# Masked copies of two experts in one VectorE instruction, in the first mixture of a two-layer kernel

## The chip, the cores and the metric

The kernel runs on one core of a Trainium2 chip. Its time is the device time of one execution in microseconds (us). Five engines work beside one another and meet through semaphores: TensorE (PE; PEld is its weight load), VectorE (DVE), ScalarE (ACT), GpSimd (POOL) and SyncE (SP), which here issues DMAs.

## What is computed

Two layers on 16 sequences of 512 tokens of 128 features. Each layer adds a gated sequence block and then a gated mixture of experts to its input, each behind a layer norm with shift and scale. The change lies in the mixture of the first layer: eight experts, one for each token.

```python
h = _layernorm(x) * (1 + cb) + sb
logits = h @ gate_w + gate_b
sel = argmax(softmax(logits))                 # one of 8 experts for each token
onehot = one_hot(sel, 8)
y_all = einsum('td,edh->eth', h, expert_w) + expert_b[:, None, :]
x = x + gb * einsum('te,eth->th', onehot, y_all)
```

## The kernel before

The kernel runs in stages with a barrier of all engines between them. The stage of the first mixture works on 16 tiles w (`B` = 16), each of 512 tokens (`C` = 4 chunks of `P` = 128 tokens). It has no loop for them: for every engine the order of its steps is written out, as `mask(0, 0); mask(0, 1); ...`, and each step waits on semaphores for what it needs. An engine does its steps strictly in that order.

For a tile the steps are these. VectorE (`statistics`, `gamma`, `joined`) and ScalarE and GpSimd (`norm_y`, `beta`, `means`, `scales`) finish the block before it and the norm; TensorE transposes the normed tokens (`turn`), ScalarE adds shift and scale and leaves the features in `f_t` (`feat`, 128 features x 512 tokens, fp32). TensorE makes the eight logits (`logits`), VectorE finds the largest and writes one-hot rows `hot` (`best`), TensorE transposes them (`turn_hot`), ScalarE writes them as `hot_b`, and SyncE sends them to DRAM and back, spread over all 128 partitions, as `wide` (128 x 8 experts x 512 tokens, bf16: one or zero for each expert and token).

Then come the masked copies and their products. `mask(w, e)` on VectorE multiplies `f_t` of the tile by the row of expert e in `wide` and writes `masked`, 128x512 fp32: the tokens of other experts are zero. `product(w, e)` on TensorE multiplies it by the weights of expert e and adds up all eight in one bank of PSUM, behind `bias(w)`. A product of fp32 is two passes, so 128 products are 256 matmul records. ScalarE scales the sum (`scaled`, into `moe_t`), TensorE transposes it back (`turn_back`), and VectorE adds it to `x_tok` (`added`).

`masked` is a ring of four buffers of one expert. `mask(w, e)` waits by `expert(dve, "product", w, e - 4)` until the product that read the same buffer last is done, and `product(w, e)` waits until the count of `masked` has passed w * 8 + e. `feat` and `spread` also wait for the last masked copy of the tile four before, as `f_t` and `wide` have four buffers.

The order of TensorE puts transposes, logits and the bias between the products, for instance `product(12, 5); product(12, 6); turn_hot(14); turn(15); product(12, 7); bias(13); logits(15); product(13, 0)`, and `turn_hot(w)` waits for `best(w)`.

Of the kernel before, what the change touches and what calls it, by code (L numbers as in the profile page):

```python
# [18 lines left out]
C = 4  # L19
# [18 lines left out]
def build(nc, a, out):  # L38
# [8 lines left out]
    with ctx:  # L47
        def sb(name, shape, dt=F32, scope=ctx):
            names_used.append(name)
            return scope.enter_context(nc.sbuf_tensor(f"{name}_{len(names_used)}", shape, dt))  # L50
# [662 lines left out]
        with ExitStack() as sc:  # L713
# [18 lines left out]
            hot_b = [sb(f"hot_b{w}", [K3, C * P], BF16, scope=sc) for w in range(W)]  # L732
            wide = [sb(f"wide{w}", [P, E, C * P], BF16, scope=sc) for w in range(W)]
            moe_t = [sb(f"moe_t{w}", [P, C * P], scope=sc) for w in range(2)]
            masked = [sb(f"masked{m}", [P, C * P], scope=sc) for m in range(4)]
            logit = sb("logit", [P, C, E], scope=sc)
            top = sb("top", [P, C, 8], scope=sc)
            idx = sb("idx", [P, C, 8], U32, scope=sc)
# [40 lines left out]
            def expert(eng, name, w, e):  # L779
                w, e = w + e // E, e % E  # L780
                if exists(w):
                    eng.wait_ge(s[name], w * E + e + 1)

            with nc.Block() as block:
# [201 lines left out]
                def _(dve):  # L986
                    def statistics(w):
                        done(dve, "y_sq", w - 1)
                        for c in range(C):
                            last = nc.vector.bn_stats(halves[:, c, :], features_of(w * C + c))  # L990
                        last.then_inc(s["y_sum"], 1)
                        done(dve, "y_sum", w)
                        for c in range(C):
                            last = nc.vector.bn_aggr(moments[:, w * C + c, :], halves[:, c, :])
                        last.then_inc(s["y_sq"], 1)

                    def stats_x(w):
                        done(dve, "joined", w)
                        done(dve, "stats_x", w - 1)
                        for c in range(C):  # L1000
                            last = nc.vector.bn_stats(halves_x[:, c, :], x_tok[:, w * C + c, :])
                        last.then_inc(s["sum_x"], 1)
                        done(dve, "sum_x", w)
                        for c in range(C):
                            last = nc.vector.bn_aggr(moments_x[:, w * C + c, :], halves_x[:, c, :])
                        last.then_inc(s["stats_x"], 1)
# [5 lines left out]
                    def gamma(w):  # L1012
                        if w < HEAD:
                            done(dve, "y_sq", w)
                            landed(dve, s_rows, w)
                            for c in range(C):
                                t = w * C + c
                                last = nc.vector.scalar_tensor_tensor(yn[w % 2][:, c, :], features_of(t), moments[:, t, 0:1], rows[w % W][:, 0, :], ALU.subtract, ALU.mult)
                            last.then_inc(s["gamma"], 1)
                        elif exists(w):  # L1020
                            done(dve, "y_normed", w)
                            landed(dve, s_rows, w)
                            nc.vector.tensor_tensor(yn[w % 2][:, :, :], yn[w % 2][:, :, :], rows[w % W][:, 0:1, :].to_broadcast([P, C, D]), ALU.mult).then_inc(s["gamma"], 1)

                    def joined(w):
                        if exists(w):
                            done(dve, "gamma", w)
                            done(dve, "beta", w)
                            if w < HEAD:
                                done(dve, "root_y", w)  # L1030
                                for c in range(C):
                                    t = w * C + c
                                    last = nc.vector.scalar_tensor_tensor(x_tok[:, t, :], yn[w % 2][:, c, :], rs_y[:, t:t + 1], x_tok[:, t, :], ALU.mult, ALU.add)
                            else:
                                for c in range(C):
                                    t = w * C + c
                                    last = nc.vector.scalar_tensor_tensor(x_tok[:, t, :], x_tok[:, t, :], 1.0, yn[w % 2][:, c, :], ALU.mult, ALU.add,
                                                                          accum_out=sum_x[:, t:t + 1])
                            last.then_inc(s["joined"], 1)
# [29 lines left out]
                    def mask(w, e):  # L1069
                        if e == 0:  # L1070
                            landed(dve, s_wide, w)
                            done(dve, "feat", w)
                        expert(dve, "product", w, e - 4)
                        nc.vector.tensor_tensor(masked[e % 4][:, :], f_t[w % W][:, :], wide[w % W][:, e, :], ALU.mult).then_inc(s["masked"], 1)  # L1074

                    dve.wait_ge(s["down"], 1)
                    statistics(0); statistics(1); gamma(0); joined(0); stats_x(0); gamma(1); shift_x_head(0); joined(1); stats_x(1)
                    statistics(2); shift_x_head(1); gamma(2); joined(2); best(0); stats_x(2); statistics(3); shift_x_head(2); best(1)
                    gamma(3); joined(3); stats_x(3); statistics(4); shift_x_head(3); mask(0, 0); mask(0, 1); mask(0, 2); mask(0, 3)
                    mask(0, 4); mask(0, 5); mask(0, 6); best(2); mask(0, 7); mask(1, 0); mask(1, 1); mask(1, 2); mask(1, 3); gamma(4)  # L1080
                    mask(1, 4); mask(1, 5); added(0); joined(4); mask(1, 6); mask(1, 7); statistics(5); statistics(6); statistics(7)
                    best(3); mask(2, 0); mask(2, 1); mask(2, 2); mask(2, 3); mask(2, 4); added(1); gamma(5); mask(2, 5); joined(5)
                    mask(2, 6); mask(2, 7); gamma(6); best(4); mask(3, 0); mask(3, 1); mask(3, 2); joined(6); mask(3, 3); mask(3, 4)
                    mask(3, 5); mask(3, 6); mask(3, 7); gamma(7); added(2); joined(7); statistics(8); best(5); mask(4, 0); mask(4, 1)
                    mask(4, 2); mask(4, 3); mask(4, 4); mask(4, 5); added(3); mask(4, 6); best(6); mask(4, 7); gamma(8); joined(8)
                    statistics(9); mask(5, 0); mask(5, 1); best(7); mask(5, 2); mask(5, 3); mask(5, 4); added(4); mask(5, 5); mask(5, 6)
                    mask(5, 7); mask(6, 0); mask(6, 1); gamma(9); mask(6, 2); joined(9); mask(6, 3); best(8); mask(6, 4); added(5)
                    mask(6, 5); statistics(10); mask(6, 6); mask(6, 7); mask(7, 0); mask(7, 1); statistics(11); mask(7, 2); best(9)
                    gamma(10); joined(10); mask(7, 3); mask(7, 4); added(6); mask(7, 5); mask(7, 6); mask(7, 7); mask(8, 0); mask(8, 1)
                    mask(8, 2); gamma(11); joined(11); mask(8, 3); mask(8, 4); mask(8, 5); added(7); statistics(12); mask(8, 6); best(10)  # L1090
                    mask(8, 7); mask(9, 0); mask(9, 1); mask(9, 2); statistics(13); gamma(12); joined(12); best(11); mask(9, 3); mask(9, 4)
                    added(8); mask(9, 5); mask(9, 6); mask(9, 7); mask(10, 0); mask(10, 1); mask(10, 2); gamma(13); joined(13); mask(10, 3)
                    mask(10, 4); mask(10, 5); best(12); added(9); statistics(14); mask(10, 6); mask(10, 7); mask(11, 0); mask(11, 1)
                    mask(11, 2); mask(11, 3); statistics(15); best(13); gamma(14); joined(14); mask(11, 4); added(10); mask(11, 5)
                    mask(11, 6); mask(11, 7); mask(12, 0); mask(12, 1); mask(12, 2); gamma(15); joined(15); mask(12, 3); mask(12, 4)
                    added(11); mask(12, 5); mask(12, 6); mask(12, 7); mask(13, 0); best(14); mask(13, 1); mask(13, 2); mask(13, 3); best(15)
                    mask(13, 4); mask(13, 5); added(12); mask(13, 6); mask(13, 7); mask(14, 0); mask(14, 1); mask(14, 2); mask(14, 3)
                    mask(14, 4); mask(14, 5); added(13); mask(14, 6); mask(14, 7); mask(15, 0); mask(15, 1); mask(15, 2); mask(15, 3)
                    mask(15, 4); mask(15, 5); added(14); mask(15, 6); mask(15, 7); added(15)

                @block.tensor
                def _(pe):
# [38 lines left out]

                    def product(w, e):
                        expert(pe, "masked", w, e)
                        nc.tensor.matmul(ps[:, w % 2, :], ew0[:, e, :], masked[e % 4][:, :], start=False, stop=(e == E - 1)).then_inc(  # L1144
                            s["product"], 1)

                    pe.wait_ge(s["weights"], 6 * 16)
# [1580 lines left out]
```

## Time and profile before

| | |
|---|---|
| three runs, us | 952.89, 949.35, 950.57 (median 950.57) |
| the profiled execution, us | 948.88 |
| its span, first to last instruction, us | 947.1 |
| mean granted TensorE clock | 0.937 of full speed |
| busy share: TensorE, VectorE, ScalarE, GpSimd | 88%, 82%, 66%, 60% |
| masked copies (line 1074), VectorE | 128, from 175.2 us to 332.4 us |
| products (line 1144), TensorE | 256 passes, 122.8 us busy |

The profile is of one execution. Times are us from its first instruction, unless marked ns. Busy time is the time in which an engine had an instruction under way. A timeline row merges like instructions: its start, the time from the first's start to the last's end, the engine, line, operation, tiles written and read, how many there are, and in brackets how long the engine stood idle before it and who released it. Successive instructions of VectorE are drawn as overlapping a little, and those of TensorE by more.

### The profile page before, as it was taken

The numbers are of one execution on the slowest core, as the hardware profiler recorded it, in microseconds if no ns is written. First come the engines' busy times: TensorE is split into PE (matmuls) and PEld (weight loads), VectorE is DVE, ScalarE is ACT, GpSimd is POOL, SyncE is SP. The second block draws the span as 40 slices with busy tenths as digits, with TensorE's granted clock in tenths as the row PEclk, the third lists the DMA queues.
The fourth block names the chain that finished last, engine by engine and source line by source line (L and its number), as shares of the span: only waits on it lengthen the run. The fifth ranks groups of instructions, "written<-read, shape, count | busy, mean of one in ns | idle before, by whom it ended". The sixth has DMA issues, their size and how long they took to land.

```text
span 947.1 us, 23545 instructions
## 1 busy us (share of the span) xinstructions
PE 833.6 (88%) x7422; PEld 645.5 (68%) x7422; DVE 775.4 (82%) x2369; ACT 629.4 (66%) x1620; POOL 570.3 (60%) x551
## 2 busy tenths in 40 slices
PE   6878892898999948999999999999729999999990
PEld 6855571444454427888888888888517888888880
DVE  3988778999999747678999999999886866666996
ACT  3567123488788365567777777766566888888880
POOL 1211004297776325343788888888777777777773
PEclk9999796799999978999999999999858999999996
DMA  5330362232322202000011111111117666756987
GB/s 155 94 95 1 90 181 63 101 145 102 146 96 90 90 25 68 2 1 10 30 36 44 39 35 37 38 36 45 44 55 219 204 208 181 223 182 195 348 250 252
DMA packets 83462, 100.79 MB, mean 106 GB/s; under 512 B 15326, under 2 KB 65305, under 8 KB 81164
## 3 DMA queue, kind: packets, MB, share of 16 engines
q1 hardware_dynamic: 71388, 79.61, 27.3%
q0 software_dynamic: 8640, 17.97, 5.3%
q10 hardware_dynamic: 3312, 1.70, 0.6%
q8 instruction: 62, 1.02, 0.5%
q14 instruction: 60, 0.49, 0.2%
HBM read 75.71 MB, written 23.54 MB: 105 GB/s over the span
## 4 chain that ended last, share of the span: by engine, by line
PE 55%; DVE 4%; DMA 1%; issue 1%; SPq 1%; ACT 1%; POOL 0%; ACTq 0%; DVEq 0%
PE ps L2636 13%; PE ps L2393 12%; PE ps L2659 7%; PE ps L2409 4%; PE ps L2471 2%; PE ps L2384 2%; PE ps L2619 2%; PE ps L2404 2%; PE ps L2530 2%; PE ps L2510 2%; PE ps L2355 1%; PE ps L2370 1%; PE ps L2458 1%; PE ps L2654 1%; PE ps L2483 1%
## 5 line engine op out<-in xcount | busy, mean ns | idle before, releaser
L1579 POOL TENSOR_TENSOR kvb<-qk,v 128x1024 f32<-128x1024 f32 x64 | 126.2, 1976 | 74.9 <-DVE qk L1950 50.3
L1588 POOL DMA_INDIRECT rows_of<-payb,posu x128 | 145.5, 1137 | 40.3 <-issue 27.8
L2393 PE MATMUL ps<-con,kvb 128*128 128x128 f32 x1024 | 126.0, 276 | 0.0
L1144 PE MATMUL ps<-masked,ew 128*128 128x512 f32 x256 | 122.8, 609 | 2.0 <-DVE masked L1074 1.9
L2393 PEld LDWEIGHTS ps<-con,kvb 128*128 128x128 f32 x1024 | 119.4, 192 | 1.0 <-issue 1.0
L2315 DVE TENSOR_SCALAR qk<-ps,b 128x256 f32<-128x256 f32 x142 | 62.0, 478 | 49.3 <-PE ps L2636 44.4
L1612 POOL DMA_INDIRECT parts<-h,dest x72 | 81.0, 1125 | 22.0 <-issue 21.0
L1926 DVE TENSOR_TENSOR qc<-ps,qk 128x1024 f32<-128x1024 f32 x64 | 78.1, 1220 | 18.4 <-PE ps L2393 17.7
L1612 POOL DMA_INDIRECT parts<-gx,dest x70 | 79.3, 1133 | 21.3 <-issue 20.7
L1074 DVE TENSOR_TENSOR masked<-f_t,wide 128x512 f32<-128x512 f32 x128 | 87.2, 725 | 5.9 <-PE ps L1144 5.7
L1144 PEld LDWEIGHTS ps<-masked,ew 128*128 128x128 f32 x256 | 44.9, 192 | 44.3 <-issue 30.4
L2659 PE MATMUL ps<-w,f_t 128*128 x568 | 75.0, 275 | 0.0
L2659 PEld LDWEIGHTS ps<-w,f_t 128*128 128x128 f32 x568 | 69.0, 192 | 8.2
L1836 ACT ACTIVATE qk<-ps,b 128x256 f32<-128x256 f32 x142 | 59.6, 471 | 18.7 <-PE ps L2636 18.3
L2636 PE MATMUL ps<-qd,ex 128*128 128x256 f32 x288 | 70.4, 388 | 0.0
L2636 PE MATMUL ps<-qd,lg 128*128 128x256 f32 x280 | 66.2, 379 | 0.0
L2636 PEld LDWEIGHTS ps<-qd,ex 128*128 128x128 f32 x288 | 53.5, 196 | 6.1
L1841 ACT ACTIVATE nrm<-qk,limit 128x512 f32<-128x512 f32 x71 | 51.3, 722 | 6.8
L2204 DVE SCALAR_TENSOR_TENSOR f_t<-qk,nrm 128x512 f32<-128x512 f32 x71 | 49.2, 693 | 6.6 <-DVE qk L2315 0.4
L2636 PEld LDWEIGHTS ps<-qd,lg 128*128 128x128 f32 x280 | 50.5, 190 | 5.4
L908 ACT ACTIVATE junk<-x_tok,stat 128x128 f32<-128x128 f32 x112 | 43.3, 389 | 12.8 <-DVE x_tok L1065 11.0
L236 POOL TENSOR_SCALAR rstd<-mv 128x16 f32<-128x16 f32 x4 | 1.1, 276 | 58.8 <-DVE mv L256 58.8
(374 smaller groups left out, 2131.1 us busy)
## 6 DMA issues: line engine op xcount, KB each, us to landing
wide<-hot_dram SPq DMA_DIRECT2D x16, 1024.0 KB, 4.5
kvb<-rows_of SPq DMA_DIRECT2D x71, 132.0 KB, 3.4
ex<-in_w_dram SPq DMA_DIRECT2D x36, 256.0 KB
lg<-in_w_dram SPq DMA_DIRECT2D x35, 256.0 KB
toep<-taps_dram SPq DMA_DIRECT2D x16, 512.0 KB, 5.0
xg<-parts SPq DMA_DIRECT2D x16, 512.0 KB, 5.9
x_tok<-in_x_dram SPq DMA_DIRECT2D x16, 256.0 KB, 3.0
rows<-rows_dram SPq DMA_DIRECT2D x16, 192.0 KB, 3.1
```

The costliest lines, as they stand in the source:

```text
L1074: nc.vector.tensor_tensor(masked[e % 4][:, :], f_t[w % W][:, :], wide[w % W][:, e, :], ALU.mult).then_inc(s["masked"], 1)
L1144: nc.tensor.matmul(ps[:, w % 2, :], ew0[:, e, :], masked[e % 4][:, :], start=False, stop=(e == E - 1)).then_inc(s["product"], 1)
L1579: nc.gpsimd.tensor_tensor(kv[g % KB][:, :, :].rearrange("p e (h d) -> p e h d", h=H), k_in, v_in, ALU.mult).then_inc(s["kv"], 1)
L1588: nc.gpsimd.indirect_dma_start(rows_of, bass.IndirectOffsetOnAxis(ap=posu[w % PR][:, slot, t:t + 1], axis=0), pay[w % PB][:, t, :], None). ...
L1612: nc.gpsimd.indirect_dma_start(parts, bass.IndirectOffsetOnAxis(ap=dest[:, at, c:c + 1], axis=0), yw[u][:, c, :], None).then_inc(s_out[u], 16)
L1836: last = nc.scalar.activation(glu[v % 2][:, f, :], ps[:, bank, f * SP:(f + 1) * SP], ACT.Relu, bias=b1[:, bass.ds(e * NF + f, 1)], scale=-1.0)
L1841: nc.scalar.activation(gs[v % 2][:, :, :], glu[v % 2][:, :, :], ACT.Gelu_apprx_sigmoid, bias=limit[:, :], scale=-1.0).then_inc(m["gs"], 1)
L1926: nc.vector.tensor_tensor(qc[g % 2][:, :, :], cum(g), q_in, ALU.mult).then_inc(s["qc"], 1)
L2315: last = nc.vector.tensor_scalar(lin[v % 2][:, f, :], ps[:, bank + 1, f * SP:(f + 1) * SP], b1[:, bass.ds(e * NF + 2 + f, 1)], 8.0, ALU.ad ...
L2393: last = nc.tensor.matmul(cum(g)[:, e, :], kv[g % KB][:, e, :], k("upto"), start=True, stop=True)
L2636: last = nc.tensor.matmul(ps[:, bank + f // 2, (f % 2) * SP:(f % 2 + 1) * SP], w1c[v % WC][:, f * P:(f + 1) * P], x_t[v % 2][:, :], start= ...
L2659: last = nc.tensor.matmul(to, act_t[v % 2][:, j, c * P:(c + 1) * P], w2[:, bass.ds(e * (2 * D) + j * D, D)], start=False, stop=(c == S - 1 ...
```

## The change

`masked` becomes two buffers of two experts (the same memory), VectorE makes the copies of experts e and e + 1 with one instruction of 2 x 512 columns, where `f_t` is repeated by a broadcast and `wide` is read over both experts. It waits for the product of expert e - 3, the second reader of its pair buffer, and counts `masked` up by 2. `product(w, e)` reads half e % 2 of pair buffer e // 2 % 2; its wait is as it was. In VectorE's written order `mask(w, e)` with odd e is gone, and stands where its even neighbour stands; all other steps keep their order. TensorE's order is as it was.

```diff
-            masked = [sb(f"masked{m}", [P, C * P], scope=sc) for m in range(4)]
+            masked = [sb(f"masked{m}", [P, 2, C * P], scope=sc) for m in range(2)]
...
                         if e == 0:
                             landed(dve, s_wide, w)
                             done(dve, "feat", w)
-                        expert(dve, "product", w, e - 4)
-                        nc.vector.tensor_tensor(masked[e % 4][:, :], f_t[w % W][:, :], wide[w % W][:, e, :], ALU.mult).then_inc(s["masked"], 1)
+                        expert(dve, "product", w, e - 3)
+                        nc.vector.tensor_tensor(masked[e // 2 % 2][:, :, :], f_t[w % W][:, :].unsqueeze(1).to_broadcast([P, 2, C * P]),
+                                                wide[w % W][:, e:e + 2, :], ALU.mult).then_inc(s["masked"], 2)
...
-                    gamma(3); joined(3); stats_x(3); statistics(4); shift_x_head(3); mask(0, 0); mask(0, 1); mask(0, 2); mask(0, 3)
-                    mask(0, 4); mask(0, 5); mask(0, 6); best(2); mask(0, 7); mask(1, 0); mask(1, 1); mask(1, 2); mask(1, 3); gamma(4)
-                    mask(1, 4); mask(1, 5); added(0); joined(4); mask(1, 6); mask(1, 7); statistics(5); statistics(6); statistics(7)
-                    best(3); mask(2, 0); mask(2, 1); mask(2, 2); mask(2, 3); mask(2, 4); added(1); gamma(5); mask(2, 5); joined(5)
...
+                    gamma(3); joined(3); stats_x(3); statistics(4); shift_x_head(3); mask(0, 0); mask(0, 2)
+                    mask(0, 4); mask(0, 6); best(2); mask(1, 0); mask(1, 2); gamma(4)
+                    mask(1, 4); added(0); joined(4); mask(1, 6); statistics(5); statistics(6); statistics(7)
+                    best(3); mask(2, 0); mask(2, 2); mask(2, 4); added(1); gamma(5); joined(5)
+                    mask(2, 6); gamma(6); best(4); mask(3, 0); mask(3, 2); joined(6); mask(3, 4)
...
+                    mask(10, 4); best(12); added(9); statistics(14); mask(10, 6); mask(11, 0)
+                    mask(11, 2); statistics(15); best(13); gamma(14); joined(14); mask(11, 4); added(10)
+                    mask(11, 6); mask(12, 0); mask(12, 2); gamma(15); joined(15); mask(12, 4)
+                    added(11); mask(12, 6); mask(13, 0); best(14); mask(13, 2); best(15)
...
-                        nc.tensor.matmul(ps[:, w % 2, :], ew0[:, e, :], masked[e % 4][:, :], start=False, stop=(e == E - 1)).then_inc(
+                        nc.tensor.matmul(ps[:, w % 2, :], ew0[:, e, :], masked[e // 2 % 2][:, e % 2, :], start=False, stop=(e == E - 1)).then_inc(
                             s["product"], 1)
```

## Rows read from the trace of the kernel before

**Rows 1.** Busy time by stretch, all engines, with granted clock and DMA
```profile
core 0: us, PE busy (x) PEld busy (x) DVE busy (x) ACT busy (x) POOL busy (x), PEclk, DMA share, GB/s
...
182.00:229.00 47.00, 42.45 (x163) 21.63 (x161) 46.04 (x175) 35.96 (x113) 33.32 (x53) 1.00 0.28 104
229.00:298.00 69.00, 67.42 (x253) 33.48 (x252) 67.42 (x258) 55.25 (x172) 50.19 (x83) 1.00 0.30 115
298.00:310.00 12.00, 11.64 (x45) 6.00 (x44) 10.53 (x35) 10.90 (x40) 8.66 (x14) 1.00 0.22 88
310.00:335.00 25.00, 25.00 (x76) 11.48 (x75) 17.91 (x51) 7.73 (x29) 8.01 (x12) 1.00 0.23 85
```

**Rows 2.** Groups: busy us, mean ns, then idle before them and its releaser
```profile
L1144 PE MATMUL ps<-masked,ew 128*128 128x512 f32 x256 | 122.8, 609 | 2.0 <-DVE masked L1074 1.9
L1074 DVE TENSOR_TENSOR masked<-f_t,wide 128x512 f32<-128x512 f32 x128 | 87.2, 725 | 5.9 <-PE ps L1144 5.7
```

**Rows 3.** Waits, 170 to 340 us: us in total, times, longest
```profile
PEld ps L1144 <- DVE masked L1074: 13.5, 36, 1.5
...
DVE masked L1074 <- PE ps L1144: 5.7, 15, 1.5
```

**Rows 4.** Timeline, start of the masked copies
```profile
175.18 2.48 DVE L1074 TENSOR_TENSOR masked<-f_t,wide 128x512 f32<-128x512 f32 x4
...
175.91 10.30 PE L1144 MATMUL ps<-masked,ew 128*128 128x512 f32 x20 [1.41 <-DVE masked L1074]
...
182.14 3.09 DVE L1074 TENSOR_TENSOR masked<-f_t,wide 128x512 f32<-128x512 f32 x5
```

**Rows 5.** Timeline, end of the stage
```profile
310.21 0.69 DVE L1074 TENSOR_TENSOR masked<-f_t,wide 128x512 f32<-128x512 f32 x1 [1.47 <-PE ps L1144]
...
311.34 1.96 PE L1144 MATMUL ps<-masked,ew 128*128 128x512 f32 x4
...
329.34 0.60 PE L1132 MATMUL ps<-con,moe_t 128*128 128x128 f32 x4
...
329.78 5.32 PE L1144 MATMUL ps<-masked,ew 128*128 128x512 f32 x12
...
330.98 1.41 DVE L1074 TENSOR_TENSOR masked<-f_t,wide 128x512 f32<-128x512 f32 x2
```

**Rows 6.** Timeline, TensorE's bias and logits ahead of the product at 311.34 us
```profile
310.11 0.39 PE L1140 MATMUL ps<-hot_b,ebx 24*128 24x512 bf16 x1
310.42 1.06 PE L1116 MATMUL ps<-gw,f_t 128*128 128x8 f32 x8
```

**Rows 7.** Timeline, VectorE, first copies of tiles 5 and 12
```profile
229.00 1.26 DVE L1074 TENSOR_TENSOR masked<-f_t,wide 128x512 f32<-128x512 f32 x2
...
298.33 1.89 DVE L1074 TENSOR_TENSOR masked<-f_t,wide 128x512 f32<-128x512 f32 x3
```

**Rows 8.** Timeline, a run of copies that meets an idle TensorE
```profile
195.99 3.09 DVE L1074 TENSOR_TENSOR masked<-f_t,wide 128x512 f32<-128x512 f32 x5
...
196.73 2.84 PE L1144 MATMUL ps<-masked,ew 128*128 128x512 f32 x6
...
199.00 0.28 DVE L1065 SCALAR_TENSOR_TENSOR x_tok<-x_tok,ps 128x128 f32<-128x128 f32 x1
```

**Rows 9.** Groups of VectorE by form, whole kernel
```profile
L1950 DVE TENSOR_TENSOR qk<-qk,lg 128x1024 f32<-128x1024 f32 x16 | 19.6, 1225 | 0.5
...
L1023 DVE TENSOR_TENSOR yn<-yn,rows 128x512 f32<-128x512 f32 x12 | 8.4, 697 | 0.0
```

**Rows 10.** Timeline, a 1024-column product of VectorE and the instruction behind it
```profile
502.58 1.23 DVE L1926 TENSOR_TENSOR qc<-ps,qk 128x1024 f32<-128x1024 f32 x1
503.72 0.94 DVE L1932 RECIPROCAL rden<-ps 96x128 f32<-96x128 f32 x1
```

**Rows 11.** Timeline, copies beside an addition of GpSimd
```profile
207.65 5.24 DVE L1074 TENSOR_TENSOR masked<-f_t,wide 128x512 f32<-128x512 f32 x5
...
208.34 1.72 POOL L867 TENSOR_TENSOR x_tok<-x_tok,rows 128x512 f32<-128x512 f32 x1
```

More of the change, by code:

```diff
@@ L1082, in _ @@
-                    best(3); mask(2, 0); mask(2, 1); mask(2, 2); mask(2, 3); mask(2, 4); added(1); gamma(5); mask(2, 5); joined(5)
-                    mask(2, 6); mask(2, 7); gamma(6); best(4); mask(3, 0); mask(3, 1); mask(3, 2); joined(6); mask(3, 3); mask(3, 4)
-                    mask(3, 5); mask(3, 6); mask(3, 7); gamma(7); added(2); joined(7); statistics(8); best(5); mask(4, 0); mask(4, 1)
-                    mask(4, 2); mask(4, 3); mask(4, 4); mask(4, 5); added(3); mask(4, 6); best(6); mask(4, 7); gamma(8); joined(8)
@@ L1086, in _ @@
[L1086 to L1097, printed above, removed]
@@ L1098, in _ @@
-                    mask(14, 4); mask(14, 5); added(13); mask(14, 6); mask(14, 7); mask(15, 0); mask(15, 1); mask(15, 2); mask(15, 3)
-                    mask(15, 4); mask(15, 5); added(14); mask(15, 6); mask(15, 7); added(15)
+                    gamma(3); joined(3); stats_x(3); statistics(4); shift_x_head(3); mask(0, 0); mask(0, 2)
+                    mask(0, 4); mask(0, 6); best(2); mask(1, 0); mask(1, 2); gamma(4)
+                    mask(1, 4); added(0); joined(4); mask(1, 6); statistics(5); statistics(6); statistics(7)
@@ new lines, in _ @@
+                    best(3); mask(2, 0); mask(2, 2); mask(2, 4); added(1); gamma(5); joined(5)
+                    mask(2, 6); gamma(6); best(4); mask(3, 0); mask(3, 2); joined(6); mask(3, 4)
+                    mask(3, 6); gamma(7); added(2); joined(7); statistics(8); best(5); mask(4, 0)
+                    mask(4, 2); mask(4, 4); added(3); mask(4, 6); best(6); gamma(8); joined(8)
+                    statistics(9); mask(5, 0); best(7); mask(5, 2); mask(5, 4); added(4); mask(5, 6)
+                    mask(6, 0); gamma(9); mask(6, 2); joined(9); best(8); mask(6, 4); added(5)
@@ new lines, in _ @@
+                    statistics(10); mask(6, 6); mask(7, 0); statistics(11); mask(7, 2); best(9)
+                    gamma(10); joined(10); mask(7, 4); added(6); mask(7, 6); mask(8, 0)
+                    mask(8, 2); gamma(11); joined(11); mask(8, 4); added(7); statistics(12); mask(8, 6); best(10)
+                    mask(9, 0); mask(9, 2); statistics(13); gamma(12); joined(12); best(11); mask(9, 4)
+                    added(8); mask(9, 6); mask(10, 0); mask(10, 2); gamma(13); joined(13)
+                    mask(10, 4); best(12); added(9); statistics(14); mask(10, 6); mask(11, 0)
@@ new lines, in _ @@
+                    mask(11, 2); statistics(15); best(13); gamma(14); joined(14); mask(11, 4); added(10)
+                    mask(11, 6); mask(12, 0); mask(12, 2); gamma(15); joined(15); mask(12, 4)
+                    added(11); mask(12, 6); mask(13, 0); best(14); mask(13, 2); best(15)
+                    mask(13, 4); added(12); mask(13, 6); mask(14, 0); mask(14, 2)
+                    mask(14, 4); added(13); mask(14, 6); mask(15, 0); mask(15, 2)
+                    mask(15, 4); added(14); mask(15, 6); added(15)
```

## The prediction

> **What bounds the kernel now.** I read the busy time by stretch first [rows 1]. The change touches one stage, the first mixture of experts, whose masked copies run from 175.2 to 332.3 us. From 182 to 298 us VectorE is busy 46.04 of 47 us and then 67.42 of 69 us, while TensorE is busy 42.45 of 47 and 67.42 of 69. From 310 us on TensorE is busy all of the 25 us and VectorE only 17.91. So VectorE carries the stage up to about 308 us, TensorE is close behind, and the end is TensorE's: it runs without a gap up to the last product.
>
> The second view is the two groups that the change touches [rows 2]: 128 masked copies by VectorE, and the 256 TensorE passes (two for each product of an expert) that read them. The third is the waits [rows 3]: VectorE's copies waited for a product for only 5.7 us in all, 15 times. The timeline places these: all lie ahead of the copies that start at 182.14 us [rows 4] or from 308.7 us on, as the one of 1.47 us that ends at 310.21 [rows 5]. Between them VectorE never waited. TensorE's weight loads waited 13.5 us for masked copies, in 36 short pieces: there VectorE is the one that is late.
>
> TensorE's own floor is near. A product of one expert is 0.86 us (twelve passes from 329.78 us hold the engine for some 5.15 us, 0.43 each), a group of four transposes 0.43 (329.34 to 329.78) [rows 5], the bias 0.31 and the logits 0.92 [rows 6]. A tile of 512 tokens needs 8 x 0.86 + 3 x 0.43 + 0.31 + 0.92 = 9.4 us. VectorE gives it one each 9.9 us: the seven tiles from 229.0 to 298.3 us [rows 7].
>
> **What the change saves.** 128 copies of 512 columns become 64 of 1024. The five copies in a row from 195.99 us have the next instruction start at 199.00, so one costs 3.01 / 5 = 0.60 us [rows 8], though each is drawn 0.68 long: successive instructions overlap by 0.08. A product of 1024 fp32 columns, both inputs in SBUF, is drawn 1225 ns [rows 9]; the nearest case of what starts behind such a one is 502.58 to 503.72 us, 1.14 [rows 10]. So a pair costs 1.14 against 1.20, and saves 0.06 us. That one input is repeated by a broadcast costs nothing extra in the nearest row: the 512-column product with broadcast rows is drawn 697 ns, beside 725 for the copies [rows 2, 9]. By drawn durations alone the saving would be 2 x 0.68 - 1.225 = 0.14; I take 0.06, since the starts are what the engine's queue pays. Over the some 50 pairs ahead of 308 us: 50 x 0.06 = 3 us. Those behind it lie beside TensorE's work and save nothing.
>
> The Trainium skill ("VectorE: DVE Perf Modes", section on the TRN2 errata) says that an SBUF-source instruction pays a fixed cost each time, and gives an fp32 tensor_tensor as N + 151 cycles. This case's drawn durations agree (0.68 and 1.225 us), its start distances don't. By that rule a pair would save 151 cycles, 0.157 us, and the 50 pairs 7.9 us.
>
> **What the change adds: waits.** The four buffers of one expert become two of two. Three things change. (1) A product of an even expert now needs the whole pair: after an idle TensorE it starts 1.22 + 0.06 us behind the pair's start, where it started 0.68 + 0.06 behind the copy's (195.99 to 196.73) [rows 8]. (2) A pair needs both products of the pair two before; a copy needed the product four before. (3) Behind a product's end the copy starts 0.20 us later (product ends at 329.78 + 1.72 = 331.50; the second copy of the row at 330.98 starts at 331.70) [rows 5].
>
> Take a run of copies that meets an idle TensorE. Before: copy k could start at 0.60 k; the fifth, at 2.41, needs the product that ends at 0.74 + 0.86 + 0.20 = 1.80, and even the seventh, at 3.61, needs one at 3.52. Seven go through without a wait. After: the third pair could start at 2.28, and needs both first products: 1.28 + 1.72 + 0.20 = 3.20. It waits 0.92 us. The order written out for VectorE has such runs of three pairs or more in nearly all tiles, across the tile's edge too (copies 6, 7 of one tile and 0 to 3 of the next). Behind the waiting pair stand the normalisation, routing and residual work of later tiles, in VectorE's queue, and behind those ScalarE, GpSimd and TensorE's transposes. As VectorE is the bound, a wait there is paid in full.
>
> I walked the two queues of the new order by hand, with these prices, the other VectorE work between pairs taken as the distance of the rows of before, and the port collisions below kept as they are. The start: the first pair is done at 176.4, the first product starts 0.55 us later (it was at 175.91), and the pairs (0, 4) and (0, 6) wait for products until 179.7 and 181.4. Before, seven copies and the routing were done by 182.14 [rows 4], the copy (1, 0) started at 182.74, and now starts at about 183.9: 1.2 us late. Then the lateness of the first copy of each tile is 1.2 at tile 2, 1.9 at tile 3 (the run at 195.99: 0.9 wait), 1.6 at 4, 2.3 at 5 and at 6, 2.7 at 7, 2.5 at 8, 3.0 at 9, 4.1 at 10, 4.5 at 11, 5.2 at 12, and 6.9 at 13, where the pair waits for product (12, 5). That last wait holds back the routing of tile 14, for which TensorE's turn of the one-hot rows stands in line: some 2 us idle. TensorE starts product (13, 0) at about 318.0, before at 311.34 [rows 5]: 6.7 us late. In sum: 1.2 us at the start, some 9 us of waits of 0.3 to 1.2 us, less 3 saved.
>
> From there TensorE has no gap, and keeps none. With product (w, 0) at time 0 pair (w, 4) may start at 1.92 and is needed at 3.9, pair (w, 6) at 4.1 and needed at 5.6. The end of the stage is therefore 6.7 us late, and nothing behind its barrier is changed.
>
> **The forecast.** The profiled execution took 948.88 us, 947.1 of them its span; 948.9 + 6.7 = 955.6. The median of the three runs is 950.57, 1.7 above the profiled one; with that offset kept, and the walk's last tenths not to be trusted, I say 957.0.
>
> **Rivals.** *Waits half absorbed.* The walk takes each wait at full price; some fall where VectorE would wait for TensorE anyway, or the collisions fall on fewer instructions. Of 9 us of waits half is left: 1.2 + 4.5 - 3 = 2.7, 953.3 us. For it speaks that TensorE has only 0.5 us of slack in a tile, against it that VectorE never waited between 182 and 308 us.
>
> *VectorE alone decides: faster.* If TensorE always kept two pairs ahead, no pair would wait, and the start's 1.2 us less the 3 saved gives -1.8: 948.8. It decides where TensorE works off each pair before VectorE has made two more; the 3.20 against 2.28 us above speaks against it. For it speaks that three copies that stood behind other work (routing, statistics) now are made with their even neighbour, 2 to 4 us sooner.
>
> *The fixed cost is the drawn one: clearly faster.* With 0.14 instead of 0.06 a pair and no waits, 50 x 0.14 - 1.2 = 5.8 off: 944.8. TensorE's idle time in 182 to 310 us, 6.5 us by its busy time [rows 1], would just allow it. The rule of the page above would make it 7.9 - 1.2 = 6.7 off, 943.9.
>
> *The port: slower still.* The five copies from 207.65 took 5.24 us instead of 3.09: GpSimd's add of 1.72 us at 208.34 and a second one each held a copy back by 1.07 [rows 11]. I keep these holds. But GpSimd's small steps, which feed the norms and so TensorE's turns, also wait for the copy under way, and would now wait up to 1.14 instead of 0.60. Some three such steps on the way to a late turn are 1.6 us, at two or three tiles: 3 to 4 us more, 960.5. The Trainium skill ("SBUF — State Buffer", section "Who interferes with whom") has VectorE with two SBUF inputs and a reading GpSimd exclude each other for a whole instruction; the collision agrees. It speaks against this change.
>
> **Chances.** Forecast (954.5 to 959.5) 0.50; half absorbed (951 to 954.5) 0.22; VectorE alone 0.11; drawn fixed cost 0.05; port 0.12. The likeliest's own range is 954.5 to 959.5. For 8 in 10 I leave out the fast end and what lies above 962: 949.5 to 962. A measurement of this kernel tells some 0.5% from no change, 4.75 us: below 945.8 faster, above 955.3 slower. Faster 0.05; same 0.22 + 0.11 and the low end of the forecast, 0.08, together 0.41; slower 0.54.
>
> **What would show it.** In the new profile: 64 copies of 1024 columns drawn near 1.23 us; VectorE's waits for products at some 15 to 18 us instead of 5.7, and many of them between 190 and 308 us, right before third pairs; VectorE no longer at 98% there; TensorE's busy share between 182 and 298 lower, its last product near 341.7 us instead of 335; 25 dense us at the end as before. The prediction is wrong if pairs start closer than 1.1 us behind one another, if VectorE's waits stay under 8 us, or if TensorE's end moves without them, which would point to GpSimd.

## The result and the profile after

The changed kernel takes 965.64 us (median of four runs, 964.22 to 966.65) against 950.56 for the kernel before: ratio 1.0148, 95% interval 1.0126 to 1.017. It is slower by 15.1 us. The sign was as forecast and the forecast waits are there; the size was not: 957.0 was said, with 954.5 to 959.5 as its own range and 962 as the top of the wide one.

The profiled execution took 964.88 us, 963.1 of them its span. In it all lines behind the changed instruction are one higher (1145 for the products). Busy time by stretch of the kernel after, to be read beside [rows 1]:

```profile
core 0: us, PE busy (x) PEld busy (x) DVE busy (x) ACT busy (x) POOL busy (x), PEclk, DMA share, GB/s
...
175.00:182.00 7.00, 5.03 (x7) 2.27 (x8) 4.16 (x10) 3.74 (x8) 4.48 (x5) 0.50 0.42 151
182.00:229.00 47.00, 41.95 (x152) 20.71 (x150) 40.42 (x142) 31.21 (x96) 32.72 (x47) 0.99 0.28 93
229.00:298.00 69.00, 60.01 (x221) 30.76 (x220) 57.93 (x201) 49.57 (x158) 50.92 (x73) 0.98 0.29 106
...
310.00:335.00 25.00, 22.86 (x83) 11.28 (x82) 18.32 (x56) 16.18 (x57) 13.19 (x19) 1.00 0.29 105
335.00:355.00 20.00, 16.96 (x48) 7.20 (x46) 11.55 (x32) 6.54 (x26) 7.00 (x11) 1.00 0.07 29
```

No engine carries the stage any more. From 229 to 298 us VectorE is busy 57.93 us instead of 67.42 and TensorE 60.01 instead of 67.42; each waits for another. GpSimd did less of its work in that time and was as busy, 50.92 us after 50.19. The groups and the busy line of the whole kernel, and the waits from 170 to 355 us, of the kernel after [rows 2, 3]:

```profile
PE 835.6 (87%) x7422; PEld 645.5 (67%) x7422; DVE 769.3 (80%) x2305; ACT 629.5 (65%) x1620; POOL 583.6 (61%) x551
...
L1145 PE MATMUL ps<-masked,ew 128*128 128x512 f32 x256 | 124.7, 618 | 3.1 <-DVE masked L1074 2.8
...
L1074 DVE TENSOR_TENSOR masked<-f_t,wide 128x1024 f32<-128x1024 f32 x64 | 79.6, 1254 | 24.8 <-PE ps L1145 24.4
```

```profile
DVE masked L1074 <- PE ps L1145: 24.4, 31, 2.8
ACT yn L932 <- POOL stat L850: 16.9, 10, 4.5
...
PE ps L1125 <- DVE hot L1056: 7.5, 7, 1.9
...
PE ps L1109 <- ACT xn L942: 7.4, 6, 4.2
```

VectorE's masked copies now wait 24.4 us for products, 5.7 before. TensorE waits 7.4 us for normed tokens to transpose (2.9 before) and 7.5 for one-hot rows (2.9 before). ScalarE waits 16.9 us for GpSimd's statistics, 8.5 before.

The timeline of the kernel after has the forecast wait at the forecast place, the run of copies at the start of tile 2 [rows 8]. VectorE:

```profile
199.75 2.36 DVE L1074 TENSOR_TENSOR masked<-f_t,wide 128x1024 f32<-128x1024 f32 x2
203.12 1.23 DVE L1074 TENSOR_TENSOR masked<-f_t,wide 128x1024 f32<-128x1024 f32 x1 [1.01 <-PE ps L1145]
204.26 0.28 DVE L1065 SCALAR_TENSOR_TENSOR x_tok<-x_tok,ps 128x128 f32<-128x128 f32 x1
```

TensorE in the same stretch: the first product 1.28 us behind the pair's start.

```profile
201.03 2.84 PE L1145 MATMUL ps<-masked,ew 128*128 128x512 f32 x6 [0.45 <-DVE masked L1074]
```

A pair costs 204.26 - 203.12 = 1.14 us, as taken, and the third of a run waits 1.01 us, where 0.92 was worked out. Two other places cost more than the walk had. The first is the start, TensorE and VectorE [rows 4]:

```profile
177.18 10.01 PE L1145 MATMUL ps<-masked,ew 128*128 128x512 f32 x16 [1.98 <-DVE masked L1074]
```

```profile
175.91 2.35 DVE L1074 TENSOR_TENSOR masked<-f_t,wide 128x1024 f32<-128x1024 f32 x2
181.06 1.23 DVE L1074 TENSOR_TENSOR masked<-f_t,wide 128x1024 f32<-128x1024 f32 x1 [2.81 <-PE ps L1145]
183.87 1.23 DVE L1074 TENSOR_TENSOR masked<-f_t,wide 128x1024 f32<-128x1024 f32 x1 [1.58 <-PE ps L1145]
```

The second is a hole in TensorE at 267 to 271.7 us, which the kernel before did not have, and behind it a stretch at the lower clock:

```profile
265.52 1.98 PE L1145 MATMUL ps<-masked,ew 128*128 128x512 f32 x4
271.66 1.01 PE L1109 MATMUL ps<-con,xn 128*128 128x128 f32 x4 [4.16 <-ACT xn L942]
```

The granted clock in both, of the kernel after (the column behind the busy times; 0.50 is 1.2 GHz, 1.00 is 2.4 GHz):

```profile
179.00:183.00 4.00, 4.00 (x6) 1.66 (x5) 1.23 (x1) 2.09 (x4) 0.65 (x2) 0.50 0.01 2
183.00:186.00 3.00, 3.00 (x8) 1.31 (x7) 2.00 (x6) 0.00 (x0) 0.00 (x0) 1.00 0.00 0
267.00:271.00 4.00, 0.50 (x2) 0.00 (x0) 2.74 (x11) 3.11 (x14) 3.15 (x5) 1.00 0.71 250
271.00:275.00 4.00, 3.34 (x10) 2.36 (x11) 1.45 (x11) 3.79 (x15) 1.79 (x5) 0.59 0.13 47
```

### The profile page after: what moved, and what is told of

Read it like the earlier page. It is cut to its first block, busy times and chain, and to the rows that moved or that the text cites. A ratio compares the mean times of both kernels' runs of the same rounds, so it can differ in the third digit from the quotient of the medians.

```text
span 963.1 us, 23543 instructions
## 1 busy us (share of the span) xinstructions
PE 835.6 (87%) x7422; PEld 645.5 (67%) x7422; DVE 769.3 (80%) x2305; ACT 629.5 (65%) x1620; POOL 583.6 (61%) x551
## 3 DMA queue, kind: packets, MB, share of 16 engines
q8 instruction: 62, 1.02, 0.4%
## 4 chain that ended last, share of the span: by engine, by line
PE 54%; DVE 3%; DMA 2%; SPq 1%; issue 1%; ACT 1%; POOL 0%; ACTq 0%; DVEq 0%; POOLq 0%
PE ps L2637 13%; PE ps L2394 12%; PE ps L2660 7%; PE ps L2410 3%; PE ps L2472 2%; PE ps L2385 2%; PE ps L2620 2%; PE ps L2405 2%; PE ps L2531 2%; PE ps L2511 2%; PE ps L2371 1%; PE ps L2356 1%; PE ps L2459 1%; DMA parts<-gx,dest 1%; PE ps L2484 1%
## 5 line engine op out<-in xcount | busy, mean ns | idle before, releaser
L1074 DVE TENSOR_TENSOR masked<-f_t,wide 128x1024 f32<-128x1024 f32 x64 | 79.6, 1254 | 24.8 <-PE ps L1145 24.4
L1613 POOL DMA_INDIRECT parts<-gx,dest x70 | 79.8, 1140 | 21.3 <-issue 20.7
L908 ACT ACTIVATE junk<-x_tok,stat 128x128 f32<-128x128 f32 x112 | 43.3, 388 | 18.0 <-DVE x_tok L1065 12.7
```

Of the source, the lines that this page charges most:

```text
L1074: nc.vector.tensor_tensor(masked[e // 2 % 2][:, :, :], f_t[w % W][:, :].unsqueeze(1).to_broadcast([P, 2, C * P]), wide[w % W][:, e:e + 2, ...
L1613: nc.gpsimd.indirect_dma_start(parts, bass.IndirectOffsetOnAxis(ap=dest[:, at, c:c + 1], axis=0), yw[u][:, c, :], None).then_inc(s_out[u], 16)
```

## The experiments

The theories. (1) The ring: with two pair buffers VectorE waits for products, and pays. (2) The long instruction: 1024 columns hold GpSimd's steps back, and the norms they feed. (3) The start: a later first product and a later clock. (4) The order: odd copies made ahead of routing and statistics delay those. The measured times are medians; each ratio is against the kernel before, measured beside it (950.57, 950.58 or 951.33 us).

**e1: four pair buffers.**

```diff
-            masked = [sb(f"masked{m}", [P, 2, C * P], scope=sc) for m in range(2)]
+            masked = [sb(f"masked{m}", [P, 2, C * P], scope=sc) for m in range(4)]
...
-                        expert(dve, "product", w, e - 3)
+                        expert(dve, "product", w, e - 7)
...
```

The copy and the product index the buffer by `(w * E + e) // 2 % 4` with it.

> The changed kernel with four pair buffers instead of two (eight experts deep), so that a pair waits for the product seven before it and no longer for the pair two before; instructions of 1024 columns and the written order stay. If the waits on the ring of buffers are the cause (theory 1), VectorE's waits for products fall from 24.4 us to under 5 and the time is 947 to 952 us, the level of before. If the 1024-column instructions holding GpSimd back are it (theory 2), GpSimd's busy time stays some 13 us above before and the time stays above 957. If the late first product and the late TensorE clock are it (theory 3), some 3 us of the 15 remain: about 954.

Measured: 960.83 us, ratio 1.0103 (1.0073 to 1.0132). The waits of e1 from 170 to 360 us and its busy line:

```profile
ACT yn L932 <- POOL stat L850: 20.1, 10, 4.5
DVE x_tok L1065 <- PE ps L1133: 15.8, 8, 4.6
...
DVE logit L1044 <- PE ps L1117: 9.1, 7, 2.3
...
PE ps L1109 <- ACT xn L942: 8.4, 5, 3.6
...
DVE masked L1074 <- PE ps L1145: 0.5, 1, 0.5
```

```profile
PE 834.3 (87%) x7407; PEld 647.3 (67%) x7422; DVE 772.3 (80%) x2305; ACT 628.7 (66%) x1620; POOL 587.5 (61%) x551
```

The ring waits are gone, 24.4 to 0.5 us, and only 4.8 of the 15 us with them. Much of that waiting came back at other steps of VectorE: it now stands 15.8 us before `added` for transposes back (7.4 in the changed kernel) and 9.1 us before `best` for logits (0.4). What is left of the loss has theory 2's mark: ScalarE waits 20.1 us for GpSimd, and GpSimd is busy 587.5 us, 17 more than before.

**e2: the pair's instruction split in two again, all its waits kept.**

```diff
-                        nc.vector.tensor_tensor(masked[e // 2 % 2][:, :, :], f_t[w % W][:, :].unsqueeze(1).to_broadcast([P, 2, C * P]),
-                                                wide[w % W][:, e:e + 2, :], ALU.mult).then_inc(s["masked"], 2)
+                        nc.vector.tensor_tensor(masked[e // 2 % 2][:, 0, :], f_t[w % W][:, :], wide[w % W][:, e, :], ALU.mult)
+                        nc.vector.tensor_tensor(masked[e // 2 % 2][:, 1, :], f_t[w % W][:, :], wide[w % W][:, e + 1, :], ALU.mult).then_inc(s["masked"], 2)
```

> The changed kernel with each 1024-column instruction split again into two of 512, and everything else as changed: the waits of a pair, its two buffers, one count of 2 behind the second, the order. Theory 1 (ring waits): nothing is won, 965 to 968 us, as the 3 us of saved fixed cost are lost too. Theory 2 (long instructions hold GpSimd): GpSimd's busy time falls back by some 13 us, TensorE's wait of 4.2 us at 267 us goes, and the time is 957 to 960.

Measured: 964.09 us, ratio 1.0143 (1.0111 to 1.0176). Its busy line:

```profile
PE 835.9 (87%) x7407; PEld 645.9 (67%) x7422; DVE 774.8 (81%) x2369; ACT 630.2 (66%) x1620; POOL 569.8 (59%) x551
```

Theory 2's signs came: GpSimd is back at 569.8 us (570.3 before), and TensorE waits 1.05 us for the norm of tile 10 (at 268.74 us) where the changed kernel has 4.16. Its gain did not come: 1.5 us by the medians, with overlapping intervals. So the hole can go and the time stay: with two pair buffers the ring (and the order) are enough for nearly the whole loss.

**e3: one expert at a time with the waits of before, in the changed order.**

```diff
-                        expert(dve, "product", w, e - 3)
...
+                        for f in (e, e + 1):
+                            expert(dve, "product", w, f - 4)
+                            nc.vector.tensor_tensor(masked[f // 2 % 2][:, f % 2, :], f_t[w % W][:, :], wide[w % W][:, f, :], ALU.mult).then_inc(s["masked"], 1)
```

> One expert at a time again, with the waits and counts of before (product four before, one count each) in four single places, but in the changed order: the copy of the odd expert right behind its even neighbour. If the order is innocent (theories 1 and 2) the time is that of before, 948 to 953 us. If pulling the odd copies ahead of routing, statistics and residual steps delays those (theory 4), it is 955 or more.

Measured: 954.22 us over ten runs, ratio 1.0028 (1.0007 to 1.0049). It is between the two expectations: the order alone costs some 2.7 us by the ratio, 0.7 to 4.7 by its interval. VectorE waits 11.1 us for products in it, 5.7 in the kernel before.

**e4: tile 0 one by one, the rest as changed.**

```diff
+                        if w == 0:
+                            for f in (e, e + 1):
+                                expert(dve, "product", w, f - 4)
+                                nc.vector.tensor_tensor(masked[f // 2 % 2][:, f % 2, :], f_t[w % W][:, :], wide[w % W][:, f, :], ALU.mult).then_inc(s["masked"], 1)
+                            return
```

> The changed kernel, but the eight copies of tile 0 are made one by one with the waits of before. Theory 3 (the start): TensorE's clock rises near 179 us as before instead of 183, VectorE starts tile 1 some 2.9 us earlier, and the time is 962 to 963 us. If the start's lateness is absorbed later in the stage: 965, no change.

Measured: 966.24 us, ratio 1.0167 (1.0134 to 1.02). Nothing is won. In the profile its first copy of tile 1 is 1.0 us later than before instead of 3.6, but that of tile 10 is 12.7 us later, as in the changed kernel: the lead is gone by then.

**e5: two instructions of 512 counted together, four pair buffers** (e2 with the ring of e1).

> Two instructions of 512 columns for a pair, counted together as in the changed kernel, but with four pair buffers. Against e2 (964.1 us, two pair buffers) it takes away the waits on the ring alone; against e3 (954.2 us) it adds that an even expert's product waits for the whole pair; against e1 (960.8 us) it has 512 columns instead of 1024. Theory 1 (ring waits are most of the loss): 954 to 957 us. If the late start of the even product is the larger part: 960 or more. Theory 2 (1024 columns hold GpSimd): at least 4 us below e1.

Measured: 954.17 us over ten runs, ratio 1.0021 (1.0003 to 1.0039). Its busy line, and TensorE at the place of the hole:

```profile
PE 832.9 (88%) x7407; PEld 645.6 (68%) x7422; DVE 773.7 (81%) x2369; ACT 629.6 (66%) x1620; POOL 567.4 (60%) x551
```

```profile
262.37 1.98 PE L1145 MATMUL ps<-masked,ew 128*128 128x512 f32 x4
265.40 0.63 PE L1109 MATMUL ps<-con,xn 128*128 128x128 f32 x4 [1.05 <-ACT xn L942]
```

This is the run that settles most. Against e2 it takes only the waits on the ring away: 9.9 us. Against e1 it differs only in the length of the instruction: 6.7 us. Against e3 it adds that an even product waits for its pair, and deeper buffers, and the two together cost nothing. That the first costs nothing by itself is not shown: e8 finds no gain in deeper buffers in the order of before, where the ring waits are 5.7 us, but in the changed order e3 has 11.1 us of them.

**e6: one exchange in GpSimd's order of the changed kernel.**

```diff
-                    ... moments_mean(10); moments_scale(10); scale_2(5); moments_mean(11)
-                    moments_scale(11); mean_x(10); ...
+                    ... moments_mean(10); moments_scale(10); moments_mean(11)
+                    moments_scale(11); scale_2(5); mean_x(10); ...
```

> The changed kernel with one exchange in GpSimd's order: its steps for the statistics of tile 11 come ahead of those for the residual of tile 5, which hold them back by some 3 us around 256 us. Theory 2 (GpSimd's stretched steps make the transpose of tile 10 late, and with it TensorE idle for 4.2 us and then at the lower clock): TensorE's wait shrinks to under 2 us, the low clock behind it goes, and the time is 960 to 963 us. Theory 1 alone: no change, 965 to 966.

Measured: 963.82 us, ratio 1.0121 (1.0089 to 1.0154), 1.8 us under the changed kernel, with overlapping intervals. TensorE's wait at the hole fell from 4.2 to 2.1 us, and the granted clock is 1.00 from 270 to 274 us, behind it.

**e7: the same exchange in e1.**

> e1 (four pair buffers, 1024 columns) with the same exchange in GpSimd's order. If ring waits and the late transpose are separate losses that add up: 955 to 957 us. If there is one chain and the time only moves to the next wait: 959 to 961.

Measured: 962.89 us, ratio 1.0115 (1.0084 to 1.0145). Neither expectation: it is not faster than e1. TensorE's wait stayed at 3.7 us. GpSimd's statistics of tile 11 were done 3.3 us sooner than in e1 (259.5 us instead of 262.8), but of the steps behind them the first and the last below then fell beside masked copies. GpSimd in e7, all before the norm of tile 10 could start:

```profile
263.52 2.21 POOL L867 TENSOR_TENSOR x_tok<-x_tok,rows 128x512 f32<-128x512 f32 x1
265.81 1.05 POOL L832 TENSOR_SCALAR stat<-stat 128x4 f32<-128x4 f32 x1
266.94 1.36 POOL L834 TENSOR_TENSOR stat<-stat,con 128x4 f32<-128x4 f32 x1
268.38 1.19 POOL L837 TENSOR_TENSOR stat<-stat,stat 128x4 f32<-128x4 f32 x1
```

The same three small steps in e1, where VectorE began its next masked copy only at 267.50 us:

```profile
267.02 0.19 POOL L832 TENSOR_SCALAR stat<-stat 128x4 f32<-128x4 f32 x1 [0.25 <-ACT junk L908]
267.30 1.16 POOL L834 TENSOR_TENSOR stat<-stat,con 128x4 f32<-128x4 f32 x1
268.54 0.23 POOL L837 TENSOR_TENSOR stat<-stat,stat 128x4 f32<-128x4 f32 x1
```

**e8: the kernel before with eight buffers.**

```diff
-            masked = [sb(f"masked{m}", [P, C * P], scope=sc) for m in range(4)]
+            masked = [sb(f"masked{m}", [P, C * P], scope=sc) for m in range(8)]
...
-                        expert(dve, "product", w, e - 4)
+                        expert(dve, "product", w, e - 8)
...
```

> The kernel before with eight buffers of one expert instead of four. It waited for its ring for 5.7 us, at the start and in TensorE's dense end. Theory 1 says a ring is worth only the waits that stand on VectorE's path, so 949.5 to 951: no change. 947 or less would say that the ring of four was already short.

Measured: 951.09 us over ten runs, ratio 1.0001 (0.9972 to 1.003). No change within 0.3%: with one expert a buffer and the order of before, four were enough.

**e9 and e10: three extra matmuls ahead of the first product,** in the changed kernel and in the kernel before.

```diff
+                    def filler():
+                        nc.tensor.matmul(ps[:, 6, :], ident, ew0[:, 0:4, :].rearrange("p e d -> p (e d)"), start=True, stop=True)
...
-                    turn(0); logits(0); turn(1); turn_hot(0); logits(1); bias(0); turn_hot(1); turn(2); bias(1); logits(2); product(0, 0)
+                    turn(0); logits(0); filler(); turn(1); turn_hot(0); logits(1); bias(0); filler(); turn_hot(1); turn(2); bias(1); logits(2); filler(); product(0, 0)
```

> The changed kernel with three extra matmuls of 512 columns, results unused, on TensorE in its idle time ahead of the first product (behind logits of tile 0, the bias of tile 0 and the logits of tile 2). Theory 3 (the start and the late clock count): the clock is at its full level at the first product or soon behind, VectorE begins tile 1 some 2 us earlier, and the time is 962 to 963.5 us. If what is won there is lost at the next wait, as in e4: 965 to 967.

> The kernel before with the same three extra matmuls. VectorE waited 1.2 us for products ahead of 182 us, at the low clock. If VectorE is the bound from there to 308 us, that is won: 949 to 950. If the fillers delay the transposes: 951 to 953.

Measured: e9 965.66 us, ratio 1.014 (1.0096 to 1.0183); e10 949.95 us over ten runs, ratio 0.9984 (0.9964 to 1.0004). e9 had its first pass all at the full clock at 181.5 us instead of 183.2, and its first copy of tile 1 at 185.5 instead of 186.3; its end is no sooner. With e4 that makes theory 3 a loss that is there at tile 1, and no part of the 15 us at the end can be seen to come from it. e10 cannot be told from no change.

**e11: work put between the pairs of a run.** At eight places of VectorE's order in the changed kernel two neighbours are exchanged, such as:

```diff
-                    best(3); mask(2, 0); mask(2, 2); mask(2, 4); added(1); gamma(5); joined(5)
+                    best(3); mask(2, 0); mask(2, 2); added(1); mask(2, 4); gamma(5); joined(5)
...
-                    mask(11, 2); statistics(15); best(13); gamma(14); joined(14); mask(11, 4); added(10)
+                    statistics(15); mask(11, 2); best(13); gamma(14); joined(14); mask(11, 4); added(10)
```

> The changed kernel (two pair buffers, 1024 columns) with eight of VectorE's steps exchanged, so that a statistics, normalisation or residual step stands between the second and third pair of a run, or between its first and second, in tiles 2, 4 and 8 to 12. Theory 1 (a pair behind two others waits 1.0 us, and VectorE pays it): VectorE's waits for products fall from 24.4 to some 17 us and the time to 959 to 962. If the waits only move: 965 to 966.

Measured: 967.72 us, ratio 1.0166 (1.0123 to 1.0208). A miss, and 2.1 us above the changed kernel. The ring waits did fall, to 20.7 us, but VectorE now stood 10.5 us (7.4 in the changed kernel) in front of `added` for TensorE's transposes back, and a wait there holds its queue as well.

**e12: e1 with the copies of tiles 7 and 8 alone in halves.**

```diff
+                        if w in (7, 8):
+                            nc.vector.tensor_tensor(masked[(w * E + e) // 2 % 4][:, 0, :], f_t[w % W][:, :], wide[w % W][:, e, :], ALU.mult)
+                            nc.vector.tensor_tensor(masked[(w * E + e) // 2 % 4][:, 1, :], f_t[w % W][:, :], wide[w % W][:, e + 1, :], ALU.mult).then_inc(s["masked"], 2)
+                            return
```

> e1 (four pair buffers, 1024 columns; 960.8 us) with the instructions of tiles 7 and 8 alone split into two of 512 columns; 56 of the 64 pairs stay as they are. Theory 2 in its place: the 1024-column copies of these two tiles stretch GpSimd's steps between 250 and 270 us, and these make the transpose of tile 10 late (TensorE's wait of 3.6 us). Then the wait falls to some 1.1 us as in e5, the lateness of tile 9 falls from +9 to +5 us, and the time is 956 to 958 us. If the stretched steps of all tiles add up, or the loss is elsewhere: 960 or more.

Measured: 959.3 us, ratio 1.0092 (1.0065 to 1.012). TensorE at the hole, in e12 and then in e1:

```profile
266.91 1.98 PE L1149 MATMUL ps<-masked,ew 128*128 128x512 f32 x4
270.55 0.63 PE L1113 MATMUL ps<-con,xn 128*128 128x128 f32 x4 [1.66 <-ACT xn L942]
```

```profile
264.99 1.99 PE L1145 MATMUL ps<-masked,ew 128*128 128x512 f32 x4
270.60 0.63 PE L1109 MATMUL ps<-con,xn 128*128 128x128 f32 x4 [3.62 <-ACT xn L942]
```

The place was right: eight pairs in halves take 2.0 us off this wait, and the low clock behind it is gone; from tile 7 to tile 9 the lateness grows by 1.1 us instead of 3.3. The size was not: 1.5 us are won in the end, with overlapping intervals, and in the profile 1.8 us of lateness come back between tiles 10 and 11, where TensorE waits for features (1.2 us at 281.3 us).

**The four kernels of length and ring,** all in the changed order and counted by pairs:

| | two pair buffers | four pair buffers |
|---|---|---|
| two instructions of 512 | 964.09 (e2) | 954.17 (e5) |
| one instruction of 1024 | 965.64 (the change) | 960.83 (e1) |

The ring alone costs 9.9 us, the length alone 6.7, both together 11.5, not 16.6. (e5 was measured beside 951.33 us for the kernel before, the others beside 950.6; by the ratios the three are 11.6, 7.8 and 12.1.) The two losses overlap. With two pair buffers the length adds only 1.5 us, which the intervals do not tell from nothing; with four it adds 6.7. The profiles show where, by how many us the first copy of a tile starts later than in the kernel before (one execution each; at tile 0 it is -1.2 to 1.2):

| | tile 1 | tile 8 | tile 9 | tile 14 |
|---|---|---|---|---|
| the change | 3.6 | 5.4 | 10.8 | 17.1 |
| e2 | 2.2 | 5.5 | 6.8 | 14.7 |
| e1 | -0.6 | 4.6 | 9.3 | 11.3 |
| e5 | -2.7 | 1.9 | 3.4 | 3.7 |

The step from tile 8 to 9, where the hole lies, comes with the long instruction in either ring (5.4 and 4.7 us against 1.3 and 1.5). The growth behind tile 9 comes with the ring of two, and e2 makes up there for part of what it was spared: 7.9 us against 6.3. Why they overlap is a reading and not shown: a VectorE that stands before its ring holds GpSimd back less. GpSimd's busy time fits it, 13.8 us more with the long instruction and two buffers (e2 to the change), 20.1 with four (e5 to e1).

## Why the prediction was wrong, point by point

- *What bounds the kernel.* Right that VectorE carried the stage: the ring alone turned 954 us into 964. Wrong that a wait there is paid in full. From e5 to e2 VectorE's ring waits rise by 20.5 us (0.5 to 21.0) and the time by 9.9, as its waits for transposes back and logits fall from 17.4 to 4.5 us.
- *A pair costs 1.14 us and saves 0.06.* Right; the start distances in the kernel after are 1.14. Neither the 0.14 of the drawn durations nor the 151 cycles of the Trainium skill's page "VectorE: DVE Perf Modes" is saved, though the drawn durations (1.23 us) fit the figure there. That rival is out.
- *The third pair of a run waits 0.92 us.* Right in mechanism and nearly in size: 1.01. The term that adds them up was too small. Between tile 1 and the first pair of tile 13 the waits for products are 12.9 us, 20 of them; the walk had some 9. That start and waits, 1.2 + 9 = 10.2 us in the sum, come so near the 9.9 us that the ring costs from e5 to e2 is partly luck: too little waiting at too high a price.
- *The start costs 1.2 us.* Too small: 3.6 - 0.7 = 2.9 us at tile 1 (the first copy itself stood 0.7 us later in this execution). The walk left TensorE's clock where it was. The clock reaches its full level within the pass that starts at 178.6 us before, and within the one at 182.5 after: the first product came later, behind 1.98 us of idle time instead of 1.41. But e4 and e9 win nothing at the end, so this is not where the time went.
- *Collisions kept as they are, GpSimd only a rival.* This is the step that failed: the sum took 3 us off for 50 shorter pairs and put nothing against it for what a longer instruction does to GpSimd's steps. The port was priced at 3 to 4 us and given 0.12, as a case beside the waits; it acts together with them. The steps from the kernel before to the changed one are by the medians +3.6 us to e5 (order, pair counting and deeper ring), +9.9 to e2 (the ring, where the sum had 10.2) and +1.5 to the change (the length, where the sum had -3). So the length is 4.5 us off in the ring of two, and 6.7 + 3 = 9.7 off in the ring of four. The rest of the miss is the 3.6, for which the sum had nothing.
- *The hole.* TensorE's wait of 4.2 us at 267 us is the length's: 4.16 and 3.62 us with 1024 columns (the change, e1), 1.05 and 1.05 with 512 (e2, e5), 1.66 with eight pairs in halves (e12). VectorE stood 3.8 us behind it, waiting for `turn_back` in the same queue; the copies of tile 9 are 10.8 us late, those of tile 8 5.4. That the shared port is the way it acts was argued from GpSimd's stretched steps and from the Trainium skill's page "SBUF — State Buffer", section "Who interferes with whom"; the steps of 0.2 us that take 1.05 to 1.19 beside pairs agree with it. No run separates that port from another thing that a long VectorE instruction might hold.
- *Order.* The walk used the new order without a price of its own, a term put at nothing. It costs some 2.7 us by e3's ratio.
- *Rivals of less or no loss.* Out as times: 953.3 and 948.8 us against 965.64, and VectorE did wait. But "waits half absorbed" had its mechanism: 20.5 us of ring waits cost 9.9. It took the half from 9 us of waits, where there were more than twice as many.
- *The dense end.* Right: the last product pass starts at 334.5 us before and at 350.7 after, as product (13, 0) starts at 327.7 us instead of 311.3 and TensorE has no gap from there. The idle time forecast ahead of it, some 2 us behind the routing of tile 14, is 1.93 us. The copies of tiles 14 and 15 are both 17.1 us late.
- *The signs named.* The copies are drawn 1.25 us, the waits rose, VectorE's share fell: all came. The waits were named as 15 to 18 us and are 24.4; the last product was named near 341.7 and ends at 351.3.

What stays open is the price of any single wait: e6, e7, e11 and e12 each went after one or a few, and half or all of the gain that was expected came back elsewhere. How much of e5's 2 to 4 us over the kernel before is the order alone is open too.

No version beat the kernel before. The best, e10, is not told from it.

## What to carry to other kernels

Merging two instructions saved only the 0.06 us a pair between their start distances, and it makes everything that synchronises on them coarser: count buffers in what one instruction fills, and if the bytes can't grow, expect the producer to lose its lead. Look also at the small GpSimd steps beside a VectorE instruction: here the longer one stretched them. Where a walk of queues finds two mechanisms that can act in different places, add their prices in the forecast before calling one a rival of the other, and test them in a two by two table, since they may overlap.

## What the runs showed of the hardware that was not expected

GpSimd's steps on four columns, 0.19 to 0.23 us beside other VectorE work, often take 0.5 to 0.6 us beside the 512-column copies (0.51 in e5 at 261.25 us, 0.60 at 258.91) and 1.05 to 1.2 beside the 1024-column ones (e1: 1.05 at 261.71, 1.20 at 262.73). One that takes 1.04 us takes 1.36 (before, at 247.13) and 2.12 (e1, at 259.51). Over the whole kernel GpSimd's busy time is 579 to 588 us in the profiles of the kernels with 1024 columns and 566 to 570 in those with 512 alone, with the same 551 instructions. And TensorE fell to 1.2 GHz within a dense stage: after the idle time of 4.2 us that ended at 271.7 us the granted clock was 0.50 from 272 to 275 us, 0.59 on the mean of 271 to 275.
